# A GNN message pass on one core: the high and low halves of a sorted group's looked-up rows are added on VectorE, and its sums have 80 rows instead of 96

## What is computed

```python
h = jnp.maximum(_layernorm(x, axis=-1), 0.0)
# feat = h, review_feat = edge_attr_64, edge_w = edge_weight1
h2 = feat @ W_node.T
rf = review_feat @ W_review.T
m = (h2[src_idx] + rf) * edge_w
rst = jax.ops.segment_sum(m, dst_idx, num_segments=N_NODES)
return x + rst
```

## Time and profile before

| | |
|---|---|
| median of 3 runs | 1810.6 us |
| the profiled execution's own time | 1820.24 us |
| its span (first to last instruction) | 1818.5 us |
| mean granted TensorE clock | 0.930 of full |
| TensorE matmul, weight load | 1564.9 us (86%), 1546.5 us (85%) |
| VectorE | 1454.8 us (80%) |
| ScalarE | 968.3 us (53%) |
| GpSimd | 1257.3 us (69%) |
| set-up until the first look-up | about 141 us |
| 15 loop iterations | about 102 us each |
| tail and output | from about 1739 us |

### The profile page before, as it was taken

The page is one execution under the profiler, slowest core; times in us unless marked ns, Lnnn a source line. Parts: engine busy times, 40 slices in busy tenths (PEclk is TensorE's granted clock), DMA queues, the critical chain, the costliest instruction groups (busy, mean ns, idle before and its releaser), DMA issues.

```text
span 1818.5 us, 75579 instructions
## 1 busy us (share of the span) xinstructions
PE 1564.9 (86%) x25040; PEld 1546.5 (85%) x25040; DVE 1454.8 (80%) x3361; ACT 968.3 (53%) x4213; POOL 1257.3 (69%) x1177
## 2 busy tenths in 40 slices
PE   0129898998989898998989898998989898998976
PEld 0029898998989898998989898998989898998975
DVE  7998886887878787877878787877878787878864
ACT  1114464655656564756646554655646554656653
POOL 2387777777777777777767677676777777776400
PEclk9659899999999999999999999999999999999965
DMA  3533354454544445454544454454444454453544
GB/s 116 87 56 94 93 118 118 97 129 94 126 97 120 109 112 123 114 123 98 116 104 114 102 122 113 111 125 98 115 105 113 104 118 117 114 130 91 121 86 51
DMA packets 513913, 195.34 MB, mean 107 GB/s; under 512 B 475071, under 2 KB 496196, under 8 KB 513212
## 3 DMA queue, kind: packets, MB, share of 16 engines
q1 hardware_dynamic: 474853, 178.88, 39.1%
q0 software_dynamic: 36000, 9.29, 6.0%
q10 hardware_dynamic: 2609, 1.55, 0.5%
HBM read 186.67 MB, written 2.92 MB: 104 GB/s over the span
## 4 chain that ended last, share of the span: by engine, by line
PE 55%; DVE 20%; issue 10%; DVEq 5%; ACT 4%; POOL 4%; DMA 1%; ACTq 0%; POOLq 0%; SPq 0%
PE found L1098 30%; PE seg L1131 13%; PE seg L1122 5%; PE edge_h L1112 4%; POOL vals_p L529 4%; DVE big L763 3%; DVE masked L817 3%; DVEq L868 2%; PE found L1106 2%; ACT mid L591 2%; DVE perm L853 2%; DVEq L860 1%; DVE masked L831 1%; DVE by_rank L708 1%; DVE by_rank L707 1%
## 5 line engine op out<-in xcount | busy, mean ns | idle before, releaser
L529 POOL DMA_INDIRECT vals_p<-h_ext,idx_t x1125 | 1238.5, 1101 | 389.8 <-issue 324.8
L1098 PE MATMUL found<-table,big 128*128 128x112 f16 (+2 forms) x16384 | 883.7, 217 | 53.1 <-DVE by_rank L881 31.8
L1098 PEld LDWEIGHTS found<-table,big 128*128 128x128 f16 x16384 | 861.4, 101 | 57.7 <-issue 57.7
L591 ACT ACTIVATE sel_p<-hit_p,wgt_t 128x64 f32<-128x64 f16 x1125 | 292.8, 335 | 518.4 <-DVE hit_p L838 516.0
L591 ACT ACTIVATE mid<-mid,wgt_t 128x64 f32<-128x64 f16 x2000 | 499.8, 333 | 112.5 <-DVE mid L838 112.5
L1131 PE MATMUL seg<-mid 128*96 128x64 f32 x4000 | 409.3, 260 | 44.1 <-ACT mid L611 39.4
L1131 PEld LDWEIGHTS seg<-mid 128*96 128x96 f32 x4000 | 387.6, 176 | 47.4 <-issue 42.5
L763 DVE TENSOR_SCALAR big<-low_all,own 128x2004 f16<-128x2004 f16 x516 | 360.2, 740 | 2.5 <-DMA low_all<-low_dram 2.5
L872 DVE SCALAR_TENSOR_TENSOR acc<-seg,count_s,acc 96x64 f32 x400 | 112.1, 280 | 174.0 <-issue 125.9
L1122 PE MATMUL seg<-sel_p,vals_p 128*80 128x64 f32 x2250 | 201.9, 237 | 5.3 <-DMA vals_p<-h_ext,idx_t 5.3
L817 DVE TENSOR_TENSOR masked<-found,mask 125x512 f32<-125x512 f32 x256 | 174.8, 683 | 32.1 <-PE found L1098 31.9
(11 more groups left out here) (131 smaller groups left out, 503.3 us busy)
## 6 DMA issues: line engine op xcount, KB each, us to landing
low_all<-low_dram SPq DMA_DIRECT2D x128, 501.0 KB
mid<-in_edge_attr_dram SPq DMA_DIRECT2D x400, 160.0 KB
vals_p<-in_edge_attr_dram SPq DMA_DIRECT2D x232, 160.0 KB
vals_p<-h_ext,idx_t POOLq DMA_INDIRECT x1125
big<-in_dst_dram SPq DMA_DIRECT2D x1, 1562.5 KB
big<-in_edge_weight_dram SPq DMA_DIRECT2D x1, 1562.5 KB
h_ext<-mid SPq DMA_DIRECT2D x2, 781.2 KB
low_all<-low_dram ACTq DMA_DIRECT2D x2, 501.0 KB
```

What stands on the lines that cost most here:

```text
L529: pool.indirect_dma_start(vals_p[:, q % RP, j, R:F], None, h_ext, bass.IndirectOffsetOnAxis(ap=idx_t[:, q * J + j:q * J + j + 1], axis=0), ...
L591: last = nc.scalar.activation(sel[:, j, :], hit[:, j, :], ACT.Copy, scale=wgt_t[:, bass.ds(tile + j, 1)])
L1098: last = nc.tensor.matmul(found[x % 2][:, r * P:r * P + n], hot[:, x // 2 % 2, a, col:col + P], rows, start=(a == 0 and part == 0), stop=( ...
```

## The change

`place_h` copies only the top 16 columns of each tile and counts a new semaphore, `top_placed`. A new VectorE function, `add_low`, waits for it, adds the 16 columns of the rest, read from PSUM, to the columns just placed, and counts `h_placed`, for which `sum_s` waits as before. So a sorted group's values have 80 columns, and `acc`, `w_rows` and `w_cols` have 80 rows; the second load of `W_node` is gone. `base_row`, which lay in row 96 of the same array, stays there under a new name, and `sq`, a temporary of the layer norm, moves into `by_rank` since `mid` is smaller.

```diff
-    FS = R + 2 * H
...
+        ROW_PART = 96
         acc_raw = sb("acc", [P, N + WINDOW])
-        acc = acc_raw[0:FS, :]
-        base_row = acc_raw[FS:FS + 1, 0:NG].bitcast(I32)
+        acc = acc_raw[0:F, :]
+        base_row = acc_raw[ROW_PART:ROW_PART + 1, 0:NG].bitcast(I32)
...
-            return seg[x % 2][0:FS, n * WINDOW:(n + 1) * WINDOW]
+            return seg[x % 2][0:F, n * WINDOW:(n + 1) * WINDOW]
...
-            sp.dma_start(w_rows[:, F:FS], w_node).then_inc(w_in, 16)
...
                     act.wait_ge(unsorted, ps * NSG + u * GROUPS + SUMS[step_of(g)][-1] + 1)
-                    nc.scalar.copy(vals_s[:, g % RS, :, R:FS],
-                                   edge_of(g).rearrange("p (q f) -> p q f", f=2 * H)).then_inc(h_placed, 1)
+                    nc.scalar.copy(vals_s[:, g % RS, :, R:F],
+                                   edge_of(g).rearrange("p (q i f) -> p q i f", i=2, f=H)[:, :, 0, :]).then_inc(top_placed, 1)
...
+                def add_low(u, g):
+
+                    dve.wait_ge(top_placed, ps * NSG + u * GROUPS + SUMS[step_of(g)][-1] + 1)
+                    parts = edge_of(g).rearrange("p (q i f) -> p q i f", i=2, f=H)
+                    nc.vector.tensor_tensor(vals_s[:, g % RS, :, R:F], parts[:, :, 1, :], vals_s[:, g % RS, :, R:F], ALU.add).then_inc(h_placed, 1)
...
                         make_hot(u, step)
+                        for g in SUMS[step]:
+                            add_low(t, g)
                         if step:
                             fold_four(u, step - 1)
...
                 for step in range(STEPS + 1):
+                    if step < STEPS:
+                        for g in SUMS[step]:
+                            add_low(u, g)
                     if step + 1 < STEPS:
```

More of the change, by code:

```diff
@@ L187, in bass_gnn_preln @@
         low_sb = by_rank_raw[:, 0:SORTED * LISTS // 2 + 1].bitcast(F16)[:, 0:SORTED * LISTS].rearrange("p (u l) -> p u l", l=LISTS)
[L190 to L193, removed]
+        mid = sb("mid", [P, RS * J * (F + WINDOW + WINDOW // 2)])
+        vals_s = mid[:, 0:RS * J * F].rearrange("p (s j f) -> p s j f", s=RS, f=F)
+        sel_s = mid[:, RS * J * F:RS * J * (F + WINDOW)].rearrange("p (s j w) -> p s j w", s=RS, w=WINDOW)
+        hit_s = mid[:, RS * J * (F + WINDOW):].bitcast(F16).rearrange("p (s j w) -> p s j w", s=RS, w=WINDOW)
         x_sb = mid[0:C, 0:NP * H].rearrange("p (i f) -> p i f", f=H)
         xc = mid[0:C, NP * H:2 * NP * H].rearrange("p (i f) -> p i f", f=H)
-        sq = mid[0:C, 2 * NP * H:3 * NP * H].rearrange("p (i f) -> p i f", f=H)
+        sq = by_rank_raw[0:C, 0:NP * H].rearrange("p (i f) -> p i f", f=H)
         temp = mid[0:C, 0:SORTED * P].rearrange("p (u j) -> p u j", j=P)
-        span_row = mid[0:1, RS * J * FS:RS * J * FS + 2 * NG].rearrange("p (k g) -> p k g", k=2)
+        span_row = mid[0:1, RS * J * F:RS * J * F + 2 * NG].rearrange("p (k g) -> p k g", k=2)
         vals_p = sb("vals_p", [P, RP, J, F])
@@ L227, in bass_gnn_preln @@
         ones = sb("ones", [P, P])
-        w_rows = sb("w_rows", [H, FS])
-        w_cols = sb("w_cols", [FS, BLOCK])
+        w_rows = sb("w_rows", [H, F])
+        w_cols = sb("w_cols", [F, BLOCK])
         span = sb("span", [C, 3, J])
@@ L298, in bass_gnn_preln @@
         unsorted = sem("unsorted")
+        top_placed = sem("top_placed")
         h_placed = sem("h_placed")
@@ L558, in _ @@
             act.wait_ge(turned, FIRST_W + 1)
-            nc.scalar.copy(w_cols[:, 0:H], turn_bank[FIRST_W % 4][0:FS, 0:H]).then_inc(placed, 1)
+            nc.scalar.copy(w_cols[:, 0:H], turn_bank[FIRST_W % 4][0:F, 0:H]).then_inc(placed, 1)
             for i, (k, m) in enumerate(rank_parts):
@@ L712, in _ @@
             assert here is key_a
-            dve.wait_ge(w_in, 48)
-            nc.vector.tensor_scalar(w_rows[:, R:FS], w_rows[:, R:FS], 1.0 / SCALE, None, ALU.mult).then_inc(w_scaled, 1)
+            dve.wait_ge(w_in, 32)
+            nc.vector.tensor_scalar(w_rows[:, R:F], w_rows[:, R:F], 1.0 / SCALE, None, ALU.mult).then_inc(w_scaled, 1)
             dve.wait_ge(made, 1)
@@ L872, in add_s @@
                     nc.vector.scalar_tensor_tensor(out=window, in0=seg_s(g),
-                                                   scalar=count_s[0:FS, 0:1], in1=window, op0=ALU.mult, op1=ALU.add).then_inc(acc_step, 1)
+                                                   scalar=count_s[0:F, 0:1], in1=window, op0=ALU.mult, op1=ALU.add).then_inc(acc_step, 1)
+                def add_low(u, g):
+                    dve.wait_ge(top_placed, ps * NSG + u * GROUPS + SUMS[step_of(g)][-1] + 1)
+                    parts = edge_of(g).rearrange("p (q i f) -> p q i f", i=2, f=H)
+                    nc.vector.tensor_tensor(vals_s[:, g % RS, :, R:F], parts[:, :, 1, :], vals_s[:, g % RS, :, R:F], ALU.add).then_inc(h_placed, 1)
                 def split_ranks(u):
@@ L1025, in _ @@
                 after(nc.vector.tensor_tensor(count_s[:], turn[:, 6:7], h_only[:], ALU.max))
-                after(nc.vector.tensor_scalar(base_row, base_row, turn[FS:FS + 1, 3:4], float(N), ALU.add, ALU.min))
+                after(nc.vector.tensor_scalar(base_row, base_row, turn[ROW_PART:ROW_PART + 1, 3:4], float(N), ALU.add, ALU.min))
                 assert nxt[0] == NEXT, nxt
@@ L1066, in _ @@
             pe.wait_ge(placed, FIRST_W - 3)
-            nc.tensor.transpose(turn_bank[FIRST_W % 4][0:FS, 0:H], w_rows[:], ident[0:H, 0:H]).then_inc(turned, 1)
+            nc.tensor.transpose(turn_bank[FIRST_W % 4][0:F, 0:H], w_rows[:], ident[0:H, 0:H]).then_inc(turned, 1)
             turns[0] += 1
```

## The result

The changed kernel takes 1936.89 us (median of 4 runs, 1932.77 to 1939.26), the kernel before 1812.16 us in the same comparison: a ratio of 1.070 (1.067 to 1.073), 125 us slower. The forecast was 1875 us with a range up to 1915. The sign was right, half of the size was missing.

What follows compares the result with a forecast made beforehand. TensorE was taken to bound a superblock's first two thirds, VectorE the last. Additions 5.0, ScalarE wait 3.9 and register load 0.8, less slack 5.4, gave +4.3 us; 15 superblocks +64, tail 0: 1875 us, range 1804 to 1915.

Steps and rivals of the forecast that it cites:

- Who bounds: In each superblock, one loop iteration of 102.18 us, TensorE limits the first two thirds and VectorE the last third.
- VectorE's slack of 5.4 us: VectorE's waits for TensorE's look-ups and last `sum_s` that added work can fill, about 5.4 us a superblock.
- A: VectorE's 400 added additions of 128 x 80, 0.20 us each, 25 a superblock: +5.0 us (4.0 to 7.0).
- B: VectorE's `add_low` waits for ScalarE's `top_placed`, mainly in steps 1 and 2: +3.9 us a superblock (1 to 5).
- D: `add_p`'s register load starts anew after a wait in `add_low`, in about half the steps: +0.8 us a superblock (0 to 2.5).
- The sum: VectorE's path in the loop: 5.0 + 3.9 + 0.8 − 5.4 of slack = +4.3 us a superblock.
- TensorE's gain of 3.0 us: `sum_s` with 80 columns instead of 96 saves 0.12 us a group, 25 groups: −3.0 us of TensorE's time a superblock.
- the tail at 0: After the loop, TensorE's shorter sums and the added work and waits were taken as 0 (−6 to +6 us).
- TensorE stays the bound: VectorE has room, so each superblock loses 3.0 us and the tail 5: 1761 us, chance 0.14.

Runs made afterwards that it cites:

- e1: Kernel before with 375 additions of 128 x 80 on VectorE, reading a constant and writing a spare array, no new wait: 1806.41 us, ratio 0.999.
- e4: Changed kernel with `add_low` moved behind `add_p` and `fold_two` in the loop: 1775.38 us, ratio 0.982 to the kernel before.
- e12: Changed kernel with ScalarE placing ahead of its sorted selections and `add_low` behind `fold_two`: 1745.23 us, ratio 0.963 to the kernel before.
- e13: Kernel before, sums of 96 columns and no addition, with ScalarE placing ahead of its sorted selections: 1770.68 us, ratio 0.976.
- e2: Kernel before with only VectorE's wait for ScalarE's placing where the change waits, no addition: 1964.88 us, ratio 1.089.
- e10: e4 with the register loads of both `add_s` of a step issued together ahead of the first: 1815.01 us, ratio 1.003 to the kernel before.
- e5: Changed kernel with ScalarE placing a step's groups earlier: ratio 1.032 to the kernel before, which took 2708.12 us beside it.
- e8: e4 with `add_low` at the very end of VectorE's step: ratio 0.995 to the kernel before, which took 2708.12 us beside it.
- e7: Kernel before with both `add_s` register loads of a step issued together: ratio 1.000 to the kernel before, which took 2708.12 us beside it.

## Why the prediction was right in sign and wrong in size

- *Who bounds, and VectorE's slack of 5.4 us*: right. e1 put the additions into it and the time didn't rise.
- *A, the additions, 5.0 us a superblock*: too high. Two start 0.29 us before the next instruction, a spacing of 0.15, so 25 × 0.15 = 3.8, just under the lower end that I had given. The Trainium skill's formula ("VectorE: DVE Perf Modes", the TRN2 errata) gave 0.24 us: the trace has 234 ns as the mean length, so it is right as a length and too high as a cost in a queue. e1 shows more: where such an addition stands in a gap it costs nothing at all.
- *B, the wait for ScalarE, 3.9 us*: right, 42.4 / 14 = 3.0. The walk through steps 1 and 2, 1.65 and 1.2 us, was close (its own figures, 830.76 + 0.2 − 829.35, give 1.61 for the first). The changed kernel's first two additions of a superblock:

```profile
880.50 0.24 DVE L879 TENSOR_TENSOR mid<-edge_h,mid 128x80 f32<-128x80 f32 x1 [1.57 <-ACT mid L611]
...
886.50 0.39 DVE L879 TENSOR_TENSOR mid<-edge_h,mid 128x80 f32<-128x80 f32 x2 [1.12 <-ACT mid L611]
```

- *D, the register load behind the wait, 0.8 us*: **this step failed**. The idle time ahead of `add_p` is 92.3 / 14 = 6.6 us an iteration, of which 0.76 stay behind step 15 as before, so D is 5.8. I had seen the mechanism and priced it as a rest of 0.1 to 0.3 us in half of the steps, by a load of 0.96 us less the work beside it, and had taken it to begin earlier wherever ScalarE was just in time. In the trace it begins when the placing is there, and the near tie between the two engines holds in nearly every step: `add_p` follows the end of the placing by 913.24 − 912.03 = 1.2 us. So it shows 178 / 14 = 12.7 times an iteration, not in half of the steps, and with 92.3 / 178 = 0.52 us each, not 0.1 to 0.3. 5.0 us too few, × 15 = 75 us. The upper end of 2.5 was too low as well, and so was the range.
- *The sum*: 3.8 + 3.0 + 5.8 − 5.4 = 7.2 of the 7.8 us measured. 0.5 of the last 0.6 us are VectorE's own work: its busy time over the 14 iterations rose from 1144.6 to 1204.8 us, 4.3 an iteration where the spacing gives 3.8. The rest is the balance of smaller waits. One of them is that for TensorE's `turn_ranks`, which ran 3.6 us at a granted clock of 0.50 in the superblock shown, behind 3.19 us of waiting, and 2.07 us at 1.00 in the one of before, behind 1.15.
- *TensorE's gain of 3.0 us and the tail at 0*: right. Two sums take 1.43 us, and the span outside the loop grew by about 1 us.
- *The rival "TensorE stays the bound"* (chance 0.14, 1761 us) describes e4, at 1775 us, and beyond it e12. The Trainium skill's rule ("Perfetto Trace Analysis", Identifying the Most-Contended Engine), to optimize the engine with the highest occupancy first, names TensorE here. e4 agrees, where the shorter sums pay 35 us; the change as made does not, 125 us slower, since the rule looks at an engine's work and not at the wait that came with the shorter sums.

Why the load doesn't start while the wait stands, whether by the wait itself or by its being against a register's value, was not tried.

## What to carry to other kernels

Ask of an added wait what stands behind it on the same engine, the register loads above all: here 3 us of waiting an iteration exposed 6 us of loads that had been hidden, and moving the addition behind `fold_four`, `add_p` and `fold_two` turned 7% slower into 1.8% faster. Near ties between two engines count as late, since the work that used to run ahead needs the signal a microsecond earlier. And cost a small operation by where it stands: 375 such additions were free in a gap. And try the order of the other engine before the change itself: placing earlier made the unchanged kernel 2.4% faster (e13), about as much as the change at its best place (e4).

## What the runs showed of the hardware

- A wait with no operation on data (e2) made the kernel 8.9% slower. A register load behind a wait of VectorE starts about 0.4 us behind the end of what it waits for (0.37 in the changed kernel, 0.45 in e2), takes 0.30 us, and the add that uses it follows the wait's end by about 1.2 us. Two loads one behind the other cost 0.88 us of idle time where one was hidden (e10).
- The kernel before took 2708 us beside e5 to e8 instead of 1811, with the same instructions. In e7, nearly the same kernel, VectorE is busy 1468 us (1455 before) and the mean granted TensorE clock is 0.79 against 0.93. Chip 13 is named for these results and for those of e12 and e13 too, beside which the kernel before took 1813 us, so the chip alone doesn't explain it. The cause is open.
